# Four subtractions of 128x1024 a pair on GpSimd instead of eight of 128x512, and route steps in halves

## The chip, the cores and the metric

One core of a Trainium2 chip runs the whole kernel. The time is device microseconds of one execution, from its start to its end; a profile of one execution lists every instruction of five engines: TensorE (PE, its weight loads as PEld), VectorE (DVE), ScalarE (ACT), GpSimd (POOL) and SyncE (SP), which only issues DMAs.

## What is computed

The reference takes `x` of 8 x 512 x 128 and computes two blocks, each with a layernorm before it and a residual after it. The first is attention with 16 heads of 64 (here with a second norm inside), the second a mixture of 64 experts, of which each token takes 8, and a shared one:

```python
x = x + attn(layernorm(x))          # scores = q.k / 8 ; attn = softmax(scores) ; ctx = attn.v ; post-norm
x = x + ffn(layernorm(x))           # route: sigmoid scores, top 4 of 8 groups, top 8 experts, weights
                                    # h = silu(x Wg) * (x Wu) * coef ; sum over experts of h Wd, plus shared
```

Products are made of 16-bit parts: a value is kept as a high part and a low part (the rest), and one product is three matmuls, high by high, high by low and low by high.

## The kernel before

The attention goes by **pairs**: 8 batches of 512 tokens by 8 pairs of heads, 64 pairs in all, numbered 0 to 63. Each engine has its own program, written out by hand; an iteration `p` of it has four slots `s` = 0 to 3, and semaphores join the engines. Pairs 0 to 11 and 28 to 63 are written out, pairs 12 to 27 are a loop (on PE and SP all are written out).

What happens to the numerators of the softmax, around which the change lies:

- PE makes the scores of pair `p` in eight pieces of 128x512 (`scores(j)`, j = 2 x key tile + head), ACT takes the exponential of each from the bank into `num` (`exponential(j)`, L723) and counts `exp_done`.
- GpSimd's `lo(s)` (L570) subtracts from `num` its upper 16 bits (`num_hi`, the same words read as bf16 with a stride of two) and writes the rest as f16 into `num_lo`. One `lo(s)` is the key tile `s`, two heads; with its second half it counts `lo_pool`.
- PE's `context(0)` of the **next** iteration multiplies by `v`; before key tile `k` it waits for `lo_pool` of that tile (`pe.wait_ge(lo_pool, 4 * (p - 1) + k + 1)`). What stands ahead of it in PE's order since the last scores of pair `p`: the product with Wo, maxima, one score piece and one projection.
- `num` and `num_lo` are rings of two pairs.

GpSimd's other work in a pair is `split_weights` after `lo(3)` (L583 or L587, by turns), and in some pairs a step of the route of block 0.

DVE makes in each pair four row maxima (L1046), the low parts of q and k (L1055), the low part of a context (L1100, 128x512, both inputs in SBUF; it belongs to pair `p - 2`), two normalisations (L1069, L1071), the low part of v (L1106) and one sum (L1085). L1100 stands behind the second row maximum of slot 2.

The **route of block 0** (layernorms, router, top 8) is spread over pairs 36 to 63 by tables: `DVE_0 = {(pair, slot): ((step, part), ...)}`, and likewise `POOL_0`, `ACT_0` and `PE_0`. `EARLY` is a place in slot 0 of DVE ahead of `low(0)`. Part `None` is a whole step, 0 and 1 are its halves (step 16: eight parts). Step 15 adds one and takes the reciprocal (128x256), step 14 on GpSimd waits for it.

The experts follow, 33 tiles for each of 8 blocks of tokens. While block `n` runs, the route of block `n + 1` is done, at the tile numbers of the tables `DVE_1`, `POOL_1`, `ACT_1`, `PE_1` (block 0) and `DVE_N`, ... (the others).

Of the kernel before, what the change touches and what calls it, by code (L numbers as in the profile page):

```python
# [18 lines left out]
P = 128  # L19
# [3 lines left out]
ALU = mybir.AluOpType  # L23
# [7 lines left out]
QT = S // P  # L31
TOK = B * S
NT = TOK // P
E, G, TOPG, TOPK = 64, 8, 4, 8
EG = E // G
# [14 lines left out]
EARLY = 4  # L50
# [1 line left out]

DVE_0 = {(36, EARLY): ((1, 0),), (36, 1): ((1, 1),), (37, 1): ((2, 0),), (38, EARLY): ((2, 1),), (38, 1): ((3, None),),
         (44, EARLY): ((7, 0),), (44, 1): ((7, 1),), (45, EARLY): ((8, None),), (48, 1): ((12, 0), (12, 1)),
         (50, EARLY): ((15, 0),), (50, 1): ((15, 1),), (52, EARLY): ((16, 0),), (52, 1): ((16, 1),), (53, EARLY): ((16, 2),),
         (53, 1): ((16, 3),), (54, EARLY): ((16, 4),), (54, 1): ((16, 5),), (55, EARLY): ((16, 6),), (55, 1): ((16, 7),),
         (56, EARLY): ((19, None),), (56, 1): ((20, 0), (20, 1)), (57, EARLY): ((21, 0),), (57, 1): ((21, 1),), (58, 1): ((23, None),),
         (59, EARLY): ((24, 0),), (59, 1): ((24, 1),), (60, EARLY): ((25, 0),), (60, 1): ((25, 1),), (61, EARLY): ((26, 0),),
         (61, 1): ((26, 1),), (62, EARLY): ((27, 0),), (62, 1): ((27, 1), (28, None))}
POOL_0 = {(37, 1): (2,), (39, 1): (3,), (42, 1): (5,), (43, 1): (6,), (45, 1): (8,), (51, 1): (14,)}  # L60
ACT_0 = {(40, 3): (4,), (41, 3): (5,), (46, 3): (9,), (47, 3): (10,), (48, 0): (11,), (49, 0): (14,), (63, 0): (30,)}
PE_0 = {(48, 0): (8,), (49, 0): (11,), (63, 0): (27,)}
# [6 lines left out]
PE_N = {8: (8,), 10: (11,), 25: (27,)}  # L69


DVE_1 = {2: (1,), 3: (2,), 4: (3,), 9: (7,), 10: (8,), 14: (12,), 18: (16,), 19: (17,), 20: (18,), 21: (19, 20), 22: (21,),
         23: (23,), 24: (24,), 25: (25,), 26: (26,), 27: (27,), 28: (28,)}
POOL_1 = {4: (3, 2), 6: (5,), 7: (6,), 10: (8,), 16: (14,)}
ACT_1 = {5: (4,), 6: (5,), 11: (9, 10), 14: (11,), 16: (14,), 31: (30,)}
PE_1 = {10: (8,), 12: (11,), 26: (27,)}


PE_TAIL_UP = {2: ((64, 0), (64, 1)), 3: ((64, 2), (64, 3))}
# [5 lines left out]
def layer(nc, x, Wq, bq, Wk, bk, Wv, bv, Wo, bo, gamma, beta, router_w, e_bias,  # L85
          Wg, Wu, Wd, SWg, SWu, SWd, out):
    with ExitStack() as ctx:  # L87
        def sem(name):
            return ctx.enter_context(nc.semaphore(name))
# [6 lines left out]
        def take(words, at=None):  # L96

            if at is None:
                at = top[0]
                top[0] += words  # L100
                assert top[0] <= ARENA, top[0]
            return arena[:, at:at + words]

        def f16(ap):
            return ap.bitcast(F16)
# [27 lines left out]
        num = num_flat.rearrange("p (r t h q) -> p r t h q", r=2, t=QT, h=2)  # L133
        num_hi = num_flat.bitcast(BF16).rearrange("p (r t h q w) -> p r t h q w", r=2, t=QT, h=2, w=2)
        numlo_at = top[0]
        num_lo = f16(take(2 * QT * 2 * S // 2)).rearrange("p (r t h q) -> p r t h q", r=2, t=QT, h=2)
# [27 lines left out]
        def tiles4(ap):  # L164
            return ap.rearrange("p (t d) -> p t d", t=QT)
# [78 lines left out]
        exp_done = sem("exp_done")  # L244
        lo_pool = sem("lo_pool")
        ctx_ps = sem("ctx_ps")
# [22 lines left out]
        sigm = sem("sigm")  # L269
# [25 lines left out]
        def halves(ap):  # L295
            rows = ap.rearrange("p t d -> p (t d)")
            return [rows[:, i * QT * E:(i + 1) * QT * E] for i in range(2)]
# [12 lines left out]
        def scores(m):  # L310
            return tiles4(halves(xin[0])[0] if m == 0 else scores_n)
# [20 lines left out]
        def wait(eng, s, value):  # L332

            if isinstance(value, int) and value <= 0:
                return
            eng.wait_ge(s, value)  # L336
# [4 lines left out]
        def valid(pair, off=0):  # L341

            return not isinstance(pair, int) or 0 <= pair + off < PAIRS
# [11 lines left out]
        def batch_of(u, batch, off):  # L355

            return (u + off) % HP, batch + (u + off) // HP
# [143 lines left out]
        def _(pool):  # L501
# [24 lines left out]
            def constants():  # L526

                pool.memset(post_eps, POST_EPS).then_inc(pool_const, 1)
                pool.memset(ln_eps, LN_EPS).then_inc(pool_const, 1)
                pool.memset(minus_one, -1.0).then_inc(pool_const, 1)  # L530
                pool.wait_ge(pool_const, 9)
# [31 lines left out]
            def run(p, u, batch):  # L563
                def lo(s):

                    for h in range(2):
                        pool.wait_ge(exp_done, 8 * p + 2 * s + h + 1)
                        if s == 0 and h == 0:
                            wait(pool, ctx_ps, 2 * (p - 2) + 2)
                        last = pool.tensor_tensor(num_lo[:, u % 2, s, h, :], num[:, u % 2, s, h, :],  # L570
                                                  num_hi[:, u % 2, s, h, :, 1], ALU.subtract)
                    last.then_inc(lo_pool, 1)

                def split_weights():

                    v, vb = batch_of(u - u % 2, batch, 2)
                    tile, half = vb * (HP // 2) + v // 2, vb * (HP // 4) + v // 4
                    dst = slice(tile, tile + 1) if isinstance(tile, int) else bass.ds(tile, 1)
                    raw = w_raw[:, v // 2 % 2:v // 2 % 2 + 1, :, :]
                    if u % 2 == 0:  # L580
                        pool.wait_ge(w_in[v // 2 % 2], (half + 1) * 48)
                        pool.wait_ge(pool_const, 6)
                        pool.tensor_copy(w_hi[:, dst, :, :], raw).then_inc(w_hi_done, 1)  # L583
                    else:
                        pool.wait_ge(w_hi_done, tile + 1)
                        pool.wait_ge(pool_const, 6)
                        pool.tensor_tensor(w_lo[:, dst, :, :], raw, w_hi[:, dst, :, :],  # L587
                                           ALU.subtract).then_inc(w_split, 1)

                for s in range(4):  # L590
                    if valid(p) and not (isinstance(p, int) and p == PAIRS - 1):
                        lo(s)
                    if isinstance(p, int) and (p, s) == (ROUTE_0, 1):
                        constants()
                    for k in block_0_at(POOL_0, p, s):
                        route(0, 0, k)
                if not isinstance(p, int) or -2 <= p - u % 2 < PAIRS:
                    split_weights()
# [12 lines left out]
            def run_block(n, r, last):  # L611
                for k in range(1, TILES if last else TILES + 1):
                    if not last:
                        for part in (POOL_N if n else POOL_1).get(k, ()):
                            route(n + 1, 1 - r, part)
# [7 lines left out]
        def _(act):  # L623
# [167 lines left out]
            def run_block(n, r, last):  # L791
                for k in range(1, TILES if last else TILES + 1):
# [6 lines left out]
                    if not last:  # L799
                        for part in (ACT_N if n else ACT_1).get(k, ()):  # L800
                            route(n + 1, 1 - r, part)
# [10 lines left out]
        def _(dve):  # L812
# [97 lines left out]
            def route(m, r, k, part=None):  # L910

                def own(ins):

                    ins.then_inc(route_step, 1)
                    n_route[0] += 1
# [8 lines left out]
                first_half, second_half = part != 1, part != 0  # L924
                some = range(QT if first_half and second_half else QT // 2) if first_half else range(QT // 2, QT)
# [25 lines left out]
                if k == 12:  # L951
                    dve.wait_ge(tr_c_hi, m + 1)
                    at = slice(some[0] * P, (some[-1] + 1) * P)
                    last = nc.vector.tensor_tensor(fT_lo[r][:, at], bank_c(m)[:, at], fT_hi[r][:, at], ALU.subtract)
# [2 lines left out]

                work1, work2, work3, work4 = work(m)
                if k == 15:
                    if first_half:  # L960
                        dve.wait_ge(logit_exp, 1)
                        nc.vector.tensor_scalar(scores(m), scores(m), 1.0, None, ALU.add).then_inc(logit_sum, 1)
                    if second_half:
                        dve.wait_ge(logit_sum, 1)
                        nc.vector.reciprocal(scores(m), scores(m)).then_inc(sigm, 1)

                g8 = sfc(m).rearrange("p t (g e) -> p (t g) e", g=G)
                n4, n2, n1 = QT * G * 4, QT * G * 2, QT * G
# [2 lines left out]
                hi1, mid1, lo1, sec1, gsum, rank = (work1[:, i * n1:(i + 1) * n1] for i in range(6))  # L971
# [36 lines left out]
                        settled()  # L1008
                        own(nc.vector.tensor_scalar(rank, rank, -2.0e38, None, ALU.is_lt))
                if k == 23:  # L1010
                    own(nc.vector.tensor_tensor(work4.rearrange("p (n e) -> p n e", e=EG), g8,
                                                rank.unsqueeze(2).broadcast_to([P, QT * G, EG]), ALU.mult))
                if k == 24:
                    for t in some:
                        own(nc.vector.max(best[:, t, :], masked[:, t, :]))
# [132 lines left out]
            def run_block(n, r, last):  # L1148
                if n == 0:
                    tail(run, DVE_TAIL[0])  # L1150
                if not last:
                    for part in (DVE_N if n else DVE_1).get(0, ()):
                        route(n + 1, 1 - r, part)
                for k in range(1, TILES if last else TILES + 1):
# [7 lines left out]
                    if not last:  # L1162
                        for part in (DVE_N if n else DVE_1).get(k, ()):
                            route(n + 1, 1 - r, part)
# [8 lines left out]
        def _(pe):  # L1173
# [262 lines left out]
            def run_block(n, r, last):  # L1436
                for k in range(1, TILES if last else TILES + 1):
# [5 lines left out]
                    if not last:  # L1443
                        for part in (PE_N if n else PE_1).get(k, ()):
                            route(n + 1, 1 - r, part)
# [53 lines left out]
```

## Time and profile before

| | |
|---|---|
| median of 3 runs | 1255.48 us (1254.57 to 1255.91) |
| the profiled execution | 1255.55 us, its span 1253.8 us |
| PE busy | 1220.3 us of the span |
| GpSimd busy | 991.7 us, of which L570 538.0 us in 504 instructions |
| DVE, ACT busy | 1066.4 us, 885.6 us |
| granted clock of TensorE | 0.989 on average; 1.00 from 50 us on |

The attention takes the span from 36 us to about 707 us, the experts the rest. A timeline row gives start, duration, engine, line, operation, target and source, and in brackets the idle time of the engine before it with what ended it. Rows of GpSimd that follow each other closely overlap a little: the next starts 0.04 us before the end of the last.

### The profile page before, as it was taken

Reading aid. Unit: us, or ns where it says so; the run is one execution under the profiler, and the core shown is the slowest. Engines: PE = TensorE matmul, PEld = TensorE weight load, DVE = VectorE, ACT = ScalarE, POOL = GpSimd, SP = SyncE. Lnnn points to the kernel's source line nnn. Section 1 sums busy time; section 2 is a strip of 40 time slices with the busy share of each in tenths; the row PEclk is TensorE's granted clock in tenths of the full one; section 3 lists DMA queues with packets and bytes.
Section 4 is the critical chain, followed back from the end, with each engine's and each line's share of the span. In section 5 each row is a group of like instructions: output and inputs, shape, how many; then the busy total and the mean of one; then the engine's idle time right before and its main releaser. Section 6 shows DMA issues by size and latency. Waiting matters only on the chain. (4 is left out here: it accounts for less than half of the span.)

```text
span 1253.8 us, 33479 instructions
## 1 busy us (share of the span) xinstructions
PE 1220.3 (97%) x12473; PEld 684.3 (55%) x12473; DVE 1066.4 (85%) x1965; ACT 885.6 (71%) x1586; POOL 991.7 (79%) x1218
## 2 busy tenths in 40 slices
PE   3999999999999999999999999999999999999998
PEld 0466666666666666666666644444444444444443
DVE  6788988888888998989999888787888878787875
ACT  4788877777777778787777666666667676667554
POOL 2788888888888999988888576868786877777665
PEclk7899999999999999999999999999999999999999
DMA  7455564665554655654565354444444444444442
GB/s 185 103 105 113 96 119 107 111 109 113 106 115 107 120 108 116 109 115 109 109 115 110 69 141 130 142 139 142 138 145 134 141 138 142 136 129 138 139 143 85
DMA packets 186862, 152.60 MB, mean 122 GB/s; under 512 B 104720, under 2 KB 143952, under 8 KB 186704
## 3 DMA queue, kind: packets, MB, share of 16 engines
q1 hardware_dynamic: 186704, 150.50, 51.1%
q8 instruction: 99, 1.62, 0.5%
q14 instruction: 59, 0.48, 0.1%
HBM read 80.16 MB, written 3.15 MB: 66 GB/s over the span
## 5 line engine op out<-in xcount | busy, mean ns | idle before, releaser
L1175 PE MATMUL bank<-arena 128*128 128x65 f16 (+2 forms) x12344 | 1209.9, 263 | 20.5 <-DVE arena L1055 7.1
L1175 PEld LDWEIGHTS bank<-arena 128*128 128x128 f16 (+1 forms) x12344 | 669.5, 98 | 548.5 <-issue 85.6
L570 POOL TENSOR_TENSOR arena<-arena 128x512 f16<-128x512 f32 x504 | 538.0, 1093 | 82.1 <-ACT arena L723 81.7
L608 POOL TENSOR_TENSOR arena<-arena 128x256 f16<-128x256 f32 x528 | 342.4, 675 | 132.3 <-ACT arena L784 125.7
L723 ACT ACTIVATE arena<-bank 128x512 f32<-128x512 f32 x512 | 291.8, 595 | 120.9 <-PE bank L1175 104.1
L1046 DVE TENSOR_REDUCE arena<-bank 128x2 f32<-128x1024 f32 x256 | 311.8, 1219 | 43.1 <-PE bank L1175 43.0
L1140 DVE TENSOR_TENSOR arena<-arena,bank 128x512 f32<-128x512 f32 x264 | 181.9, 689 | 61.9 <-ACT bank L779 38.9
L784 ACT ACTIVATE arena<-arena 128x512 f16<-128x512 f32 x264 | 164.7, 624 | 95.9 <-DVE arena L1140 94.0
L1132 DVE TENSOR_TENSOR arena<-arena,bank 128x512 f32<-128x512 f32 x256 | 173.9, 679 | 24.2 <-PE bank L1175 23.2
L779 ACT ACTIVATE bank<-bank 128x512 f32<-128x512 f32 x264 | 153.3, 581 | 55.3 <-PE bank L1175 55.1
L1055 DVE SCALAR_TENSOR_TENSOR arena<-bank,arena 128x512 f16<-128x512 f32 x128 | 95.5, 746 | 19.4 <-ACT arena L713 19.3
L713 ACT ACTIVATE arena<-bank,arena 128x512 f16<-128x512 f32 x128 | 87.9, 687 | 20.7 <-PE bank L1175 16.3
L748 ACT ACTIVATE arena<-bank 2x1024 f16<-2x1024 f32 x64 | 65.0, 1015 | 11.0 <-PE bank L1175 10.8
L1100 DVE TENSOR_TENSOR arena<-arena 128x512 f16<-128x512 f32 x64 | 63.6, 994 | 2.6 <-ACT arena L756 2.6
L1071 DVE TENSOR_TENSOR arena<-bank,arena 128x256 f32<-128x256 f32 x128 | 54.3, 425 | 4.4
L1106 DVE TENSOR_TENSOR arena<-bank,arena 128x512 f16<-128x512 f32 x64 | 43.6, 681 | 0.5 <-ACT arena L764 0.5
L1085 DVE TENSOR_TENSOR arena<-bank,arena 128x512 f32<-128x512 f32 (+1 forms) x64 | 43.6, 681 | 0.0
L756 ACT ACTIVATE arena<-arena 128x512 f16<-128x512 f32 x64 | 39.8, 622 | 3.5 <-DMA arena<-arena 3.5
L764 ACT ACTIVATE arena<-bank 128x512 f16<-128x512 f32 x64 | 39.1, 611 | 0.0
L587 POOL TENSOR_TENSOR arena<-arena 128x384 f16<-128x384 f32 (+1 forms) x33 | 30.2, 915 | 0.2
L740 ACT ACTIVATE arena<-arena 128x8 f16<-128x8 f32 x64 | 13.5, 210 | 23.8 <-DVE arena L1046 23.7
L1069 DVE RECIPROCAL arena<-bank 128x4 f32<-128x4 f32 x128 | 22.8, 178 | 4.1 <-PE bank L1175 2.8
(106 smaller groups left out, 368.0 us busy)
## 6 DMA issues: line engine op xcount, KB each, us to landing
arena<-coef_rows SPq DMA_DIRECT2D x512, 128.0 KB, 2.9
arena<-arena SPq DMA_DIRECT2D x256, 128.0 KB, 2.5
arena<-arena SPq DMA_DIRECT2D x64, 256.0 KB, 3.1
arena<-in_L_attn_x SPq DMA_DIRECT2D x9, 256.0 KB, 3.5
arena<-in_L_ffn_Wg SPq DMA_DIRECT2D x32, 64.0 KB, 2.4
arena<-in_L_ffn_Wu SPq DMA_DIRECT2D x32, 64.0 KB, 2.2
arena<-in_L_ffn_Wd SPq DMA_DIRECT2D x32, 64.0 KB, 2.2
arena<-arena SPq DMA_TRANSPOSE x128, 3.4
```

Of the source, the lines that this page charges most:

```text
L570: last = pool.tensor_tensor(num_lo[:, u % 2, s, h, :], num[:, u % 2, s, h, :], num_hi[:, u % 2, s, h, :, 1], ALU.subtract)
L608: last = pool.tensor_tensor(hid_lo[:, r, at], hid[:, r, at], hid_hi[:, r, at], ALU.subtract)
L713: nc.scalar.activation(flat[:, (u + 3) % 2, (ZQH, ZKH)[which], :], proj_bank(t, which), ACT.Identity, bias=bias[:, n:n + 1]).then_inc(qk_h ...
L723: nc.scalar.activation(num[:, u % 2, j // 2, j % 2, :], ps_st[ST_BANK[j]], ACT.Exp).then_inc(exp_done, 1)
L748: nc.scalar.activation(stack[K:K + 2, (u + 1) % 4, :, Q2, :], ps_turn[K:K + 2, :].unsqueeze(1).broadcast_to([2, 2, S]), ACT.Copy).then_inc ...
L779: nc.scalar.activation(ps_gate[r % 3], ps_gate[r % 3], ACT.Silu).then_inc(silu_done, 1)
L784: nc.scalar.activation(hid_hi[:, r, :], hid[:, r, :], ACT.Copy).then_inc(hid_hi_done, 1)
L1046: nc.vector.tensor_reduce(rmax[:, up % 2, q, :], max_bank(pair, q).rearrange("p (h k) -> p h k", h=2), AX.X, ALU.max).then_inc(max_done, 1)
L1055: nc.vector.scalar_tensor_tensor(out=flat[:, (u + 3) % 2, (ZQL, ZKL)[which], :], in0=proj_bank(t, which), scalar=(bq8, bk_c)[which][:, n:n ...
L1132: nc.vector.tensor_tensor(prod[:, i % 2, :], coef_b[:, j % 4, :], ps_up[i % 3], ALU.mult).then_inc(prod_done, 1)
L1140: nc.vector.tensor_tensor(hid[:, i % 6, :], prod[:, i % 2, :], ps_gate[i % 3], ALU.mult).then_inc(hid_done, 1)
L1175: return nc.tensor.matmul(out_, lhsT, rhs, start=start, stop=stop, skip_group_check=True)
```

## The change

`lo(s)` becomes one instruction over both heads, 128x1024, which waits for the exponential of the second head; before, each head had an instruction and a wait of its own. Step 15 of block 0 gets three parts, the reciprocal in two halves of 128x128, in pairs 50 and 51. Step 23 of block 0 is halved, step 28 moves by a slot. In `DVE_1`, `POOL_1`, `ACT_1` and `PE_1` steps 4 to 14 move by one tile (step 4 from tile 5 to 6, and so on).

```diff
-         (50, EARLY): ((15, 0),), (50, 1): ((15, 1),), (52, EARLY): ((16, 0),), ...
+         (50, EARLY): ((15, 0),), (50, 1): ((15, 1),), (51, EARLY): ((15, 2),), (52, EARLY): ((16, 0),), ...
...
-POOL_1 = {4: (3, 2), 6: (5,), 7: (6,), 10: (8,), 16: (14,)}
+POOL_1 = {4: (3, 2), 7: (5,), 8: (6,), 11: (8,), 17: (14,)}
...
-                    for h in range(2):
-                        pool.wait_ge(exp_done, 8 * p + 2 * s + h + 1)
-                        if s == 0 and h == 0:
-                            wait(pool, ctx_ps, 2 * (p - 2) + 2)
-                        last = pool.tensor_tensor(num_lo[:, u % 2, s, h, :], num[:, u % 2, s, h, :],
-                                                  num_hi[:, u % 2, s, h, :, 1], ALU.subtract)
-                    last.then_inc(lo_pool, 1)
+                    pool.wait_ge(exp_done, 8 * p + 2 * s + 2)
+                    if s == 0:
+                        wait(pool, ctx_ps, 2 * (p - 2) + 2)
+                    pool.tensor_tensor(num_lo[:, u % 2, s, :, :], num[:, u % 2, s, :, :],
+                                       num_hi[:, u % 2, s, :, :, 1], ALU.subtract).then_inc(lo_pool, 1)
...
                 if k == 15:
-                    if first_half:
+                    if part == 0:
                         dve.wait_ge(logit_exp, 1)
                         nc.vector.tensor_scalar(scores(m), scores(m), 1.0, None, ALU.add).then_inc(logit_sum, 1)
-                    if second_half:
+                    else:
+                        half = scores(m)[:, (part - 1) * QT // 2:part * QT // 2, :]
                         dve.wait_ge(logit_sum, 1)
-                        nc.vector.reciprocal(scores(m), scores(m)).then_inc(sigm, 1)
+                        last = nc.vector.reciprocal(half, half)
+                        if part == 2:
+                            last.then_inc(sigm, 1)
```

GpSimd's order in two of the written-out pairs before, with the semaphores each waits for (L583 and L587 are `split_weights`, L570 is `lo`):

```order
L583 CAST arena<-arena 128x384 [waits pool_const,w_in0]
L570 TENSOR_TENSOR arena<-arena 128x512 [waits ctx_ps,exp_done]
L570 TENSOR_TENSOR arena<-arena 128x512 [waits exp_done] x7
L587 TENSOR_TENSOR arena<-arena 128x384 [waits pool_const,w_hi_done]
L570 TENSOR_TENSOR arena<-arena 128x512 [waits ctx_ps,exp_done]
```

The same place now (L581 and L585 are `split_weights`, L569 is `lo`):

```order
L581 CAST arena<-arena 128x384 [waits pool_const,w_in1]
L569 TENSOR_TENSOR arena<-arena 128x1024 [waits ctx_ps,exp_done]
L569 TENSOR_TENSOR arena<-arena 128x1024 [waits exp_done] x3
L585 TENSOR_TENSOR arena<-arena 128x384 [waits pool_const,w_hi_done]
L569 TENSOR_TENSOR arena<-arena 128x1024 [waits ctx_ps,exp_done]
```

Nothing else moves on GpSimd in the attention: four instructions with four waits stand where eight with eight stood.

DVE's order from slot 1 of pair 50 on, before (L965 is the reciprocal of step 15, L1046 a row maximum, L1055 `low`, L1085 the sum):

```order
L965 RECIPROCAL arena<-arena 128x256
L1046 TENSOR_REDUCE arena<-bank 128x2
L1055 SCALAR_TENSOR_TENSOR arena<-bank,arena 128x512
L1046 TENSOR_REDUCE arena<-bank 128x2
L1100 TENSOR_TENSOR arena<-arena 128x512
L1069 RECIPROCAL arena<-bank 128x4
L1071 TENSOR_TENSOR arena<-bank,arena 128x4x64
L1106 TENSOR_TENSOR arena<-bank,arena 128x512
L1046 TENSOR_REDUCE arena<-bank 128x2
L1085 TENSOR_TENSOR arena<-bank,arena 128x512
L1055 SCALAR_TENSOR_TENSOR arena<-bank,arena 128x512
```

And now (L964 is the reciprocal; the other lines stand two further down in the file than before):

```order
L964 RECIPROCAL arena<-arena 128x128
L1048 TENSOR_REDUCE arena<-bank 128x2
L1057 SCALAR_TENSOR_TENSOR arena<-bank,arena 128x512
L1048 TENSOR_REDUCE arena<-bank 128x2
L1102 TENSOR_TENSOR arena<-arena 128x512
L1071 RECIPROCAL arena<-bank 128x4
L1073 TENSOR_TENSOR arena<-bank,arena 128x4x64
L1108 TENSOR_TENSOR arena<-bank,arena 128x512
L1048 TENSOR_REDUCE arena<-bank 128x2
L1087 TENSOR_TENSOR arena<-bank,arena 128x512
L964 RECIPROCAL arena<-arena 128x128
L1057 SCALAR_TENSOR_TENSOR arena<-bank,arena 128x512
```

Half of the reciprocal has moved ten instructions on, into slot 0 of pair 51.

## Rows read from the trace of the kernel before

**Rows 1.** The page, part 1: busy time of each engine.

```profile
PE 1220.3 (97%) x12473; PEld 684.3 (55%) x12473; DVE 1066.4 (85%) x1965; ACT 885.6 (71%) x1586; POOL 991.7 (79%) x1218
```

**Rows 2.** Windows: length, then busy PE, PEld, DVE, ACT, POOL; clock, DMA share, GB/s.

```profile
40.00:705.00 665.00, 661.94 (x9605) 424.49 (x9603) 596.69 (x901) 512.83 (x919) 582.62 (x580) 1.00 0.56 108
720.00:1170.00 450.00, 447.69 (x2247) 209.49 (x2246) 373.96 (x891) 299.76 (x544) 340.75 (x531) 1.00 0.46 138
```

**Rows 3.** Timeline, ACT: the first exponential of pairs 38 to 41.

```profile
441.65 0.60 ACT L723 ACTIVATE arena<-bank 128x512 f32<-128x512 f32 x1 [1.21 <-PE bank L1175]
...
452.19 0.60 ACT L723 ACTIVATE arena<-bank 128x512 f32<-128x512 f32 x1 [1.21 <-PE bank L1175]
...
462.73 0.60 ACT L723 ACTIVATE arena<-bank 128x512 f32<-128x512 f32 x1 [1.21 <-PE bank L1175]
...
473.44 0.60 ACT L723 ACTIVATE arena<-bank 128x512 f32<-128x512 f32 x1 [0.45 <-PE bank L1175]
```

**Rows 4.** Timeline, GpSimd: last four subtractions of pair 38, then of pair 39.

```profile
448.34 4.49 POOL L570 TENSOR_TENSOR arena<-arena 128x512 f16<-128x512 f32 x4 [1.18 <-ACT arena L723]
...
458.03 1.02 POOL L541 TENSOR_TENSOR arena<-arena 128x4 f32<-128x4 f32 x1
...
459.28 4.48 POOL L570 TENSOR_TENSOR arena<-arena 128x512 f16<-128x512 f32 x4
```

**Rows 5.** Groups of GpSimd by form: count, busy us, mean ns, idle before.

```profile
L570 POOL TENSOR_TENSOR arena<-arena 128x512 f16<-128x512 f32 x504 | 538.0, 1093 | 82.1 <-ACT arena L723 81.7
...
L547 POOL TENSOR_TENSOR arena<-arena 128x512 f32<-128x512 f32 x8 | 10.2, 1280 | 0.0
...
L556 POOL TENSOR_TENSOR arena<-arena 128x256 f32<-128x256 f32 x8 | 5.8, 724 | 2.8 <-PE bank L1175 1.6 <-ACT arena L696 1.2
...
L543 POOL TENSOR_TENSOR arena<-arena 128x4 f32<-128x4 f32 x16 | 3.2, 201 | 1.3
```

**Rows 6.** Timeline, GpSimd: pieces 4, 5 and 7 of pair 30.

```profile
363.69 1.04 POOL L570 TENSOR_TENSOR arena<-arena 128x512 f16<-128x512 f32 x1 [1.18 <-ACT arena L723]
...
364.70 1.48 POOL L570 TENSOR_TENSOR arena<-arena 128x512 f16<-128x512 f32 x1
...
367.14 1.04 POOL L570 TENSOR_TENSOR arena<-arena 128x512 f16<-128x512 f32 x1
```

**Rows 7.** Timeline, ACT: exponentials 5 and 7 of pair 30.

```profile
364.03 0.59 ACT L723 ACTIVATE arena<-bank 128x512 f32<-128x512 f32 x1
...
365.73 0.60 ACT L723 ACTIVATE arena<-bank 128x512 f32<-128x512 f32 x1
```

**Rows 8.** Timeline, DVE: L1100 in pair 30 and in pair 58.

```profile
364.31 0.97 DVE L1100 TENSOR_TENSOR arena<-arena 128x512 f16<-128x512 f32 x1
...
662.26 0.68 DVE L1100 TENSOR_TENSOR arena<-arena 128x512 f16<-128x512 f32 x1
```

**Rows 9.** Timeline of ACT, DVE and GpSimd in pair 24, inside the loop.

```profile
300.81 0.59 ACT L723 ACTIVATE arena<-bank 128x512 f32<-128x512 f32 x1
...
301.02 1.03 DVE L1100 TENSOR_TENSOR arena<-arena 128x512 f16<-128x512 f32 x1
...
300.47 4.49 POOL L570 TENSOR_TENSOR arena<-arena 128x512 f16<-128x512 f32 x4 [1.18 <-ACT arena L723]
```

**Rows 10.** Timeline: first exponentials of pairs 50 and 51, the reciprocal, PE's wait.

```profile
569.24 0.60 ACT L723 ACTIVATE arena<-bank 128x512 f32<-128x512 f32 x1 [1.21 <-PE bank L1175]
...
573.16 1.74 DVE L965 RECIPROCAL arena<-arena 128x256 f32<-128x256 f32 x1
...
576.04 0.39 PE L1175 MATMUL bank<-arena 128*128 128x512 f16 x1 [0.82 <-DVE arena L1046]
...
580.76 0.60 ACT L723 ACTIVATE arena<-bank 128x512 f32<-128x512 f32 x1 [1.21 <-PE bank L1175]
```

**Rows 11.** Waits: PE for L570 (us in total, times, longest).

```profile
PE bank L1175 <- POOL arena L570: 0.9, 2, 0.6
```

**Rows 12.** The page, part 5: DVE's row maxima.

```profile
L1046 DVE TENSOR_REDUCE arena<-bank 128x2 f32<-128x1024 f32 x256 | 311.8, 1219 | 43.1 <-PE bank L1175 43.0
```

More of the change, by code:

```diff
@@ L54 @@
          (44, EARLY): ((7, 0),), (44, 1): ((7, 1),), (45, EARLY): ((8, None),), (48, 1): ((12, 0), (12, 1)),
-         (50, EARLY): ((15, 0),), (50, 1): ((15, 1),), (52, EARLY): ((16, 0),), (52, 1): ((16, 1),), (53, EARLY): ((16, 2),),
+         (50, EARLY): ((15, 0),), (50, 1): ((15, 1),), (51, EARLY): ((15, 2),), (52, EARLY): ((16, 0),), (52, 1): ((16, 1),), (53, EARLY): ((16, 2),),
          (53, 1): ((16, 3),), (54, EARLY): ((16, 4),), (54, 1): ((16, 5),), (55, EARLY): ((16, 6),), (55, 1): ((16, 7),),
-         (56, EARLY): ((19, None),), (56, 1): ((20, 0), (20, 1)), (57, EARLY): ((21, 0),), (57, 1): ((21, 1),), (58, 1): ((23, None),),
+         (56, EARLY): ((19, None),), (56, 1): ((20, 0), (20, 1)), (57, EARLY): ((21, 0),), (57, 1): ((21, 1),), (58, EARLY): ((23, 0),), (58, 1): ((23, 1),),
          (59, EARLY): ((24, 0),), (59, 1): ((24, 1),), (60, EARLY): ((25, 0),), (60, 1): ((25, 1),), (61, EARLY): ((26, 0),),
-         (61, 1): ((26, 1),), (62, EARLY): ((27, 0),), (62, 1): ((27, 1), (28, None))}
+         (61, 1): ((26, 1),), (62, EARLY): ((27, 0),), (62, 1): ((27, 1),), (62, 2): ((28, None),)}
 POOL_0 = {(37, 1): (2,), (39, 1): (3,), (42, 1): (5,), (43, 1): (6,), (45, 1): (8,), (51, 1): (14,)}
@@ L69 @@
 PE_N = {8: (8,), 10: (11,), 25: (27,)}
-DVE_1 = {2: (1,), 3: (2,), 4: (3,), 9: (7,), 10: (8,), 14: (12,), 18: (16,), 19: (17,), 20: (18,), 21: (19, 20), 22: (21,),
+DVE_1 = {2: (1,), 3: (2,), 4: (3,), 10: (7,), 11: (8,), 15: (12,), 18: (16,), 19: (17,), 20: (18,), 21: (19, 20), 22: (21,),
          23: (23,), 24: (24,), 25: (25,), 26: (26,), 27: (27,), 28: (28,)}
-POOL_1 = {4: (3, 2), 6: (5,), 7: (6,), 10: (8,), 16: (14,)}
-ACT_1 = {5: (4,), 6: (5,), 11: (9, 10), 14: (11,), 16: (14,), 31: (30,)}
-PE_1 = {10: (8,), 12: (11,), 26: (27,)}
+POOL_1 = {4: (3, 2), 7: (5,), 8: (6,), 11: (8,), 17: (14,)}
+ACT_1 = {6: (4,), 7: (5,), 12: (9, 10), 15: (11,), 17: (14,), 31: (30,)}
+PE_1 = {11: (8,), 13: (11,), 26: (27,)}
 PE_TAIL_UP = {2: ((64, 0), (64, 1)), 3: ((64, 2), (64, 3))}
@@ L1010, in route @@
                 if k == 23:
-                    own(nc.vector.tensor_tensor(work4.rearrange("p (n e) -> p n e", e=EG), g8,
-                                                rank.unsqueeze(2).broadcast_to([P, QT * G, EG]), ALU.mult))
+                    at = slice(some[0] * G, (some[-1] + 1) * G)
+                    own(nc.vector.tensor_tensor(work4.rearrange("p (n e) -> p n e", e=EG)[:, at, :], g8[:, at, :],
+                                                rank[:, at].unsqueeze(2).broadcast_to([P, len(some) * G, EG]), ALU.mult))
                 if k == 24:
```

## The prediction

> **What bounds the kernel now.** I read the busy times first, then stretches of the span, then single pairs. PE is busy 1220.3 of 1253.8 us [rows 1]; in the attention 661.94 of 665.00 us, in the experts 447.69 of 450.00 us, at a granted clock of 1.00 [rows 2]. GpSimd is the next busiest there only after DVE, with 582.62 us of 665.00. So PE sets the pace, and a pair costs what PE's own instructions cost: its first exponential starts 10.54 us after that of the pair before (441.65 to 452.19 to 462.73 [rows 3]). Less work on GpSimd gives PE nothing back, since in the whole run PE stands visibly still for L570 twice, 0.9 us together [rows 11]. What can matter is when the last subtraction of a pair ends, because PE needs it in the next iteration.
>
> How much later may it end? The trace has a trial of it. In pair 38 the last piece ends at 448.34 + 4.49 = 452.83, which is 11.18 us after that pair's first exponential. In pair 39 a route step on GpSimd (L541, 1.02 us) stands ahead, and the last piece ends at 459.28 + 4.48 = 463.76, 11.57 us after 452.19 [rows 3, 4]: 0.39 us later. The next distance of first exponentials is 473.44 - 462.73 = 10.71 instead of 10.54, so PE lost 0.17 us. About 0.22 us of delay is free, the rest is paid one to one. And it is paid in every pair in which it happens: what GpSimd waits for comes from PE, so a late subtraction delays PE, which delays the next exponentials by the same.
>
> **The change part by part.**
>
> *The length of a piece.* No row shows 128x1024. A piece of 512 alone takes 1.04 us [rows 6]. An instruction of 4 elements takes 0.20 us; of the f32 forms, 512 and 256 elements take 1.28 and 0.72 us, which puts 0.17 us outside the elements [rows 5]. So 0.17 to 0.20 of the 1.04 us is there once per instruction, and a merged piece saves that: 2 x 1.04 - 0.19 = 1.89 us. The bounds are 1.88 (all of the 0.20 saved) and 2.04 (nothing saved; two pieces back to back, which overlap by 0.04). I take 1.89, which both neighbours give. GpSimd's busy time falls by about 252 x 0.15 = 38 us, all of it time in which PE didn't wait.
>
> *When the last piece ends, written-out pairs.* Pair 30 as it is: exponential 5 ends at 364.03 + 0.59 = 364.62, piece 4 (started 363.69, after exponential 4) ends at 364.73, piece 5 ends at 366.18, piece 7 at 368.18 [rows 6, 7]. Piece 5 takes 1.48 us instead of 1.04, and that is L1100: DVE starts it at 364.31 while piece 4 runs, and it ends at 365.28, 0.55 us after piece 4; piece 5 ends 0.90 us after L1100 [rows 6, 8]. The two don't overlap: DVE stood until piece 4 was done, then piece 5 until L1100 was done, with 0.14 us of its 1.04 already behind it. The Trainium skill has a rule on these two ("SBUF — State Buffer", section "SBUF: two separate sides"): GpSimd and a VectorE instruction with two SBUF inputs share a port pair, whichever starts first holds it for the whole instruction. The trace agrees, with the 0.97 us of L1100 and the 1.48 us beside it. The rule speaks against the change, since one hold by GpSimd grows from 1.04 to 1.89 us; a sum by that is a rival below.
>
> Now the new order. Pieces 2 and 3 used to end at 363.69 - 1.18 = 362.51. The first two merged pieces start where piece 1 did, with the second head's exponential, and take 3.74 instead of 3.04 us: they end near 363.2. The third must wait for exponential 5, so GpSimd is idle when L1100 comes at 364.31. L1100 runs at once, 0.68 us as in pair 58 where it hardly waited [rows 8], to 364.99. The third piece, released at 364.70, is held until then and ends at 364.99 + 1.89 - 0.14 = 366.74. The fourth starts 0.04 us earlier, at 366.70 (exponential 7 ended at 366.33 [rows 7], so it isn't what holds it), and ends at 368.59. That is 0.41 us later than 368.18; 0.22 are free, so PE loses 0.19 us a pair.
>
> The reason in a word: half of the old work of key tile 2 was done before exponential 5 was there. Now none of it can be, and the saved 0.19 us a piece doesn't make up for it.
>
> *In the loop.* Pair 24: exponential 5 ends at 301.40, L1100 starts at 301.02, the last piece ends at 300.47 + 4.49 = 304.96 [rows 9]. New: L1100 to 301.70, third piece to 303.45, fourth to 305.30, 0.34 us later; PE loses 0.12 us.
>
> *Behind the later piece* on GpSimd stand `split_weights` and the first piece of the next pair. The next first piece waits for its own exponentials, over a microsecond later, and the weights are needed by the experts alone, so nothing else is late. The waits for the second head in the first two pieces cost nothing: PE takes tiles 0 and 1 a whole iteration later.
>
> *Reciprocal.* In pair 50 it holds DVE for 1.74 us, PE stands 0.82 us for the row maximum behind it, and the pair takes 580.76 - 569.24 = 11.52 us [rows 10]. In halves DVE is late by some 0.9 us less at that place, which is the whole wait. Pair 50 becomes a pair like the others: 10.54 + 0.19 - 11.52 = -0.79 us. The second half, in slot 0 of pair 51, stands ahead of a `low` and a row maximum; DVE has idle time there in the mean (43.1 us over 64 pairs, 0.67 a pair [rows 12]), and a rest of 0.2 us disappears in PE's new wait.
>
> *Other steps of the route.* Step 23 in halves and step 28 a slot later: the same DVE work. The steps of block 1, one tile later: PE's whole idle time from 720 to 1170 us is 2.3 us [rows 2], so not more than that can be gained; a GpSimd step of 1.28 us [rows 5] put ahead of an awaited tile would cost at most about that. I take 0.
>
> *Sum.* Written-out pairs 3 to 11 and 28 to 59 without pair 50: 40 x 0.19 = 7.6. Loop, pairs 12 to 27: 16 x 0.12 = 1.9. Pairs 1, 2 and 60 to 62: the last three have no projection ahead of the context, so no slack, and pay up to 0.41 each; five pairs at 0.3 make 1.5. Pair 50: -0.8. Together +10.2 us on the profiled execution's 1255.55 (span 1253.8 and 1.75 around it), which is 0.07 from the median of the runs: 1265.7 us, 0.8% slower.
>
> **The rivals.**
>
> *The hold by L1100 costs nothing* (GpSimd gets the port at once or L1100 shifts away). Then the third piece ends at 364.70 + 1.89 = 366.59, the fourth at 368.44, 0.26 us late, 0.04 paid: 56 x 0.04 + 5 x 0.2 - 0.95 = +2.3, so 1257.9 us. For it: DVE will have a little more idle time. Against it: 0.44 us of hold in piece 5 in pair after pair, and L1100's start is bound to PE like everything else.
>
> *It is faster or nothing changes*: the slack is larger than 0.22 us or the merged piece shorter than 1.78 us. Then the pairs stay at 10.54 us, PE's own work, and only pair 50 gains: 1255.55 - 0.98 = 1254.6 us. A gain of more than 2.5 us would need other waits to vanish with it, which only the experts' 2.3 us could supply. Against it: 0.20 us is all that an instruction can save.
>
> *Merged pieces save nothing*, 2.04 us each. The last piece is another 0.30 us later: 40 x 0.49 + 16 x 0.42 + 5 x 0.6 - 0.5 = +28.8, so 1284 us. The Trainium skill ("GPSIMD Engine Reference", section "Elementwise — side-by-side cycle accounting") gives 4497 ns for a two-input add over 2048 f32 and about 2.5 cycles an element as a floor; an estimate from it is 2.25 us a piece, and about 1310 us. The trace differs for this form: 1.04 us for 512 elements is below that floor, so the row decides.
>
> *DVE is shut out by a long piece.* If L1100 came after the third piece's start, 0.39 us later than now (364.31 against 364.70), it would wait to 366.59 and end at 367.14 instead of 365.28. DVE would be 1.86 us late a pair against 0.67 idle [rows 12], 1.2 us a pair over 60 pairs: about 1327 us. The port rule named above speaks for this one: a lock held for 1.89 us is worse to meet than one of 1.04. Against it: both starts hang on the same PE work, so the 0.39 us should stay. In pairs 36 to 62 single route steps on DVE may meet a long piece; that is inside my range.
>
> **How the numbers follow.** Forecast 0.60; no hold 0.18; nothing or faster 0.10; nothing saved 0.07; DVE shut out 0.05. A measurement of this kernel tells about 0.2%, 2.5 us, from no change. Slower: the forecast, the two slow rivals and 0.08 of the second case, whose 1257.9 lies on the border: 0.80. The same: 0.10 of it and half of the third: 0.15. Faster: 0.05. The likeliest case's own range is 1261 to 1271 (0.03 us more or less a piece moves a pair by 0.06, the sum by 4). The range for all, 1257 to 1277, takes in the second case and half of the way to pieces that save nothing.
>
> **What would show it.** GpSimd's group of 252 instructions of 128x1024 at about 1.9 us, held ones a little longer; L1100 near 0.68 us instead of 0.97; first exponentials 10.73 us apart in the written-out pairs and 10.66 in the loop; pair 50 no longer at 11.52. PE's new waits are so short that few will be listed as idle time. It would be wrong if the pairs stayed at 10.54, or if the third piece ran 1.9 us from its release with L1100 at 0.97 or more.

## The result, and the profile after

The changed kernel takes 1265.93 us (median of 4 runs, 1265.41 to 1266.27) against 1255.70 of the kernel before: a ratio of 1.0083, 95% interval 1.0071 to 1.0096. The forecast was 1265.7. The profiled execution took 1266.27 us, its span 1264.5, which is 10.7 us more than before.

The page's busy times, to set beside [rows 1]:

```profile
PE 1229.1 (97%) x12473; PEld 687.7 (54%) x12473; DVE 1049.1 (83%) x1967; ACT 889.3 (70%) x1586; POOL 938.1 (74%) x966
```

GpSimd is busy 54 us less, DVE 17 us less, and the kernel is slower. Neither engine's busy time was what the time hung on. The attention's stretch (columns as in [rows 2]) hardly shows it either: PE is idle for 675.00 - 670.16 = 4.84 us of it, against 3.06 us before.

```profile
40.00:715.00 675.00, 670.16 (x9602) 427.80 (x9600) 577.63 (x898) 515.96 (x919) 527.77 (x328) 1.00 0.54 106
```

The loss shows in the distance of pairs. First exponentials of pairs 30 and 31 (written out), 24 and 25 (loop), 50 and 51, from the timeline of ACT:

```profile
361.63 0.60 ACT L721 ACTIVATE arena<-bank 128x512 f32<-128x512 f32 x1 [1.21 <-PE bank L1177]
...
372.36 0.60 ACT L721 ACTIVATE arena<-bank 128x512 f32<-128x512 f32 x1 [1.21 <-PE bank L1177]
...
297.50 0.60 ACT L721 ACTIVATE arena<-bank 128x512 f32<-128x512 f32 x1 [1.15 <-PE bank L1177]
...
308.17 0.60 ACT L721 ACTIVATE arena<-bank 128x512 f32<-128x512 f32 x1 [1.15 <-PE bank L1177]
...
577.76 0.60 ACT L721 ACTIVATE arena<-bank 128x512 f32<-128x512 f32 x1 [1.21 <-PE bank L1177]
...
588.49 0.60 ACT L721 ACTIVATE arena<-bank 128x512 f32<-128x512 f32 x1 [1.21 <-PE bank L1177]
```

10.73 us written out, 10.67 in the loop, 10.73 for pair 50; before it was 10.54, 10.54 and 11.52 [rows 3, 10]. Inside pair 30, the third and fourth merged piece, DVE's L1102 (L1100 before) and exponential 5:

```profile
369.52 2.05 POOL L569 TENSOR_TENSOR arena<-arena 128x1024 f16<-128x1024 f32 x1 [1.53 <-ACT arena L721]
...
371.53 1.89 POOL L569 TENSOR_TENSOR arena<-arena 128x1024 f16<-128x1024 f32 x1
...
369.13 0.68 DVE L1102 TENSOR_TENSOR arena<-arena 128x512 f16<-128x512 f32 x1
...
368.85 0.59 ACT L721 ACTIVATE arena<-bank 128x512 f32<-128x512 f32 x1
```

A piece alone takes 1.89 us, as forecast; the third is held to 2.05 by L1102, which comes first and takes 0.68 instead of 0.97 us [rows 8]. The last piece ends at 373.42, 3.98 us after exponential 5 (369.44). Before it was 368.18 - 364.62 = 3.56 [rows 6, 7]: 0.42 us later, of which 0.19 shows in the distance of pairs. (From the pair's first exponential, at 361.63, the last piece is 0.61 us later than before. The other 0.19 is the stop of the pair before: it lies ahead of exponential 5 and isn't lateness of GpSimd.) GpSimd now waits 1.53 us for exponential 5, in front of the chain that matters.

The list of waits hides nearly all of it. PE for L569 (us in total, times, longest), to set beside [rows 11]:

```profile
PE bank L1177 <- POOL arena L569: 1.9, 6, 0.7
```

Six waits of 1.9 us are listed, while some sixty pairs each lost 0.13 to 0.19 us. The ends of matmuls are modelled, and the small ones of `context` overlap in the listing, so most of a short stop is hidden. The matmul that needs pair 30's last piece starts 0.06 us after the piece's end (373.42), and the row ahead of it ends at 372.53 + 0.92 = 373.45:

```profile
372.53 0.92 PE L1177 MATMUL bank<-arena 128*128 128x512 f16 x19
...
373.48 0.29 PE L1177 MATMUL bank<-arena 128*128 128x65 f16 x4
```

A stop of 0.19 us shows as a gap of 0.03 us, too short for the list. The distance of a repeating event is the view that shows such a loss.

Where the 10.7 us are, by the distances of first exponentials in the two timelines:

| stretch | longer by, us | the forecast's term |
|---|---|---|
| pairs 3 to 11 | 2.0 | 9 x 0.19 = 1.7 |
| pairs 12 to 27 (loop) | 2.2 | 16 x 0.12 = 1.9 |
| pairs 28 to 59 without 50 | 5.7 | 31 x 0.19 = 5.9 |
| pair 50 | -0.8 | -0.8 |
| pairs 1, 2 and 60 to 62 | 1.7 | 1.5 |
| start, pair 63, experts | -0.1 | 0 |

### The profile page after: what moved, and what is told of

It is laid out like the page before. It is cut to its first block and busy times, and to the rows that moved or that the text cites. A ratio compares the mean times of both kernels' runs of the same rounds, so it can differ in the third digit from the quotient of the medians.

```text
span 1264.5 us, 33165 instructions
## 1 busy us (share of the span) xinstructions
PE 1229.1 (97%) x12473; PEld 687.7 (54%) x12473; DVE 1049.1 (83%) x1967; ACT 889.3 (70%) x1586; POOL 938.1 (74%) x966
## 5 line engine op out<-in xcount | busy, mean ns | idle before, releaser
L569 POOL TENSOR_TENSOR arena<-arena 128x1024 f16<-128x1024 f32 x252 | 481.4, 1929 | 146.9 <-ACT arena L721 145.8
L1048 DVE TENSOR_REDUCE arena<-bank 128x2 f32<-128x1024 f32 x256 | 311.7, 1218 | 51.1 <-PE bank L1177 50.7
L1102 DVE TENSOR_TENSOR arena<-arena 128x512 f16<-128x512 f32 x64 | 44.1, 688 | 4.1 <-ACT arena L754 4.1
L585 POOL TENSOR_TENSOR arena<-arena 128x384 f16<-128x384 f32 (+1 forms) x33 | 30.3, 920 | 0.2
L681 ACT ACTIVATE arena<-arena 128x128 f32<-128x128 f32 x32 | 13.3, 482 | 17.1 <-POOL arena L543 17.1
```

Of the source, the lines that this page charges most:

```text
L569: pool.tensor_tensor(num_lo[:, u % 2, s, :, :], num[:, u % 2, s, :, :], num_hi[:, u % 2, s, :, :, 1], ALU.subtract).then_inc(lo_pool, 1)
L1048: nc.vector.tensor_reduce(rmax[:, up % 2, q, :], max_bank(pair, q).rearrange("p (h k) -> p h k", h=2), AX.X, ALU.max).then_inc(max_done, 1)
```

## The experiments

### Each half of the change alone

The first is the kernel before with the merged `lo` and nothing else of the change:

```diff
-                    for h in range(2):
-                        pool.wait_ge(exp_done, 8 * p + 2 * s + h + 1)
...
+                    pool.wait_ge(exp_done, 8 * p + 2 * s + 2)
...
```

The second is the changed kernel with the old `lo`:

```diff
-                    pool.wait_ge(exp_done, 8 * p + 2 * s + 2)
...
+                    for h in range(2):
+                        pool.wait_ge(exp_done, 8 * p + 2 * s + h + 1)
...
```

> The kernel before with the merged subtractions alone; tables and reciprocal as before. Theory (the late last piece is the whole loss, the route tables bring only pair 50's 0.8 to 1.0 us): 1266.6 us, pairs 10.73 us apart (loop 10.66), pair 50 still the longest at 11.3 to 11.7. Rival (the moved route steps cost part of the 10 us): clearly under 1265, the pairs between 10.54 and 10.73.

> The change without the merging: eight subtractions of 128x512 a pair, but the new tables, the reciprocal in halves and step 23 in halves. Theory: pairs 10.54 us apart as before, pair 50 too, so 1255.55 - 0.98 = 1254.6 us. Rival (the moved steps cost something themselves): 1257 us or more, with new waits of PE between pair 36 and the first 20 tiles of experts.

The merging alone took 1267.25 us, 1.0101 of before (1.0084 to 1.0117); the tables alone 1254.69 us, 0.9998 (0.9989 to 1.0008). So all of the loss comes with the merging, and what the tables bring is under what whole runs can tell. In the traces the pairs of the first stand 10.73 us apart (10.67 in the loop), those of the second 10.54. Pair 50 takes 11.33 us in the first and 578.70 - 567.98 = 10.72 us in the second:

```profile
567.98 0.60 ACT L723 ACTIVATE arena<-bank 128x512 f32<-128x512 f32 x1 [1.22 <-PE bank L1179]
...
578.70 0.60 ACT L723 ACTIVATE arena<-bank 128x512 f32<-128x512 f32 x1 [1.22 <-PE bank L1179]
```

That is 0.18 us over the 10.54 that was expected of it. In the whole change pair 50 takes 10.73, like its neighbours: there this rest of the reciprocal's cost and the 0.19 us of the late piece don't add up. The tables also cost something that was expected to be free: pair 62 takes 8.92 us with them alone and 8.59 before.

With the merging alone, pair 50 shows something the forecast had only as a rival. DVE is late there from the long reciprocal, and L1098 (its L1100) comes after the third piece has started:

```profile
585.77 1.90 POOL L569 TENSOR_TENSOR arena<-arena 128x1024 f16<-128x1024 f32 x1 [1.56 <-ACT arena L721]
...
586.09 2.12 DVE L1098 TENSOR_TENSOR arena<-arena 128x512 f16<-128x512 f32 x1
```

It stands until the piece ends at 587.67 and finishes 0.54 us later: 2.12 us instead of 0.68. This is DVE shut out by a long piece, in one pair of this kernel. In the whole change the halved reciprocal keeps DVE from being so late, and it doesn't occur in pair 50.

### Which merged piece costs

Both are the changed kernel with a `lo(s)` that does some tiles in one subtraction and the others in two. The first merges tiles 0, 1 and 3, the second tile 2 alone (there the condition is `s in (2,)`):

```diff
+                    if s in (0, 1, 3):
+                        pool.wait_ge(exp_done, 8 * p + 2 * s + 2)
...
+                    else:
+                        for h in range(2):
+                            pool.wait_ge(exp_done, 8 * p + 2 * s + h + 1)
...
```

> The change, but key tile 2 again in two subtractions of 128x512; tiles 0, 1 and 3 stay merged. Theory (the loss is the head start lost on tile 2 before exponential 5): piece 4 starts with exponential 4 again, tile 2 is done 366.18 - 357.00 = 9.18 us after the pair's first exponential as before, the merged tile 3 is released by exponential 7 (9.33 + 0.08) and ends at 11.30, 0.12 later than before and inside the 0.22 of slack: pairs 10.54 us apart, about 1255.0 us. Rival (every merged piece costs by its own length or its late release): three quarters of the loss, about 1263 us, pairs at 10.68.

> The change, but only key tile 2 merged; tiles 0, 1 and 3 in two subtractions each. Theory: tile 2 ends 9.74 us after the pair's first exponential, the two halves of tile 3 follow back to back and take 2.00 instead of 1.85: the last ends 0.56 us later than before in the written-out pairs and 0.49 in the loop, of which 0.34 and 0.27 are paid. Slower than the whole change: pairs about 10.88 us apart (loop 10.81), 40 x 0.34 + 16 x 0.27 + some 2 - 0.6 = +19, about 1275 us. Rival (cost by merged piece): a quarter of the loss, about 1257 us.

Tile 2 merged alone: 1274.41 us, 1.0158 (1.0141 to 1.0175), and slower than all four merged. Three merged but not tile 2: 1257.09 us, 1.0017 (1.0008 to 1.0027). A cost by the number of merged pieces would have had them the other way round. GpSimd and first exponentials of pairs 30 and 31 with tile 2 merged alone:

```profile
365.40 0.60 ACT L730 ACTIVATE arena<-bank 128x512 f32<-128x512 f32 x1 [1.21 <-PE bank L1186]
...
376.27 0.60 ACT L730 ACTIVATE arena<-bank 128x512 f32<-128x512 f32 x1 [1.21 <-PE bank L1186]
...
373.43 2.05 POOL L570 TENSOR_TENSOR arena<-arena 128x1024 f16<-128x1024 f32 x1 [1.97 <-ACT arena L730]
...
375.44 2.03 POOL L577 TENSOR_TENSOR arena<-arena 128x512 f16<-128x512 f32 x2
```

and the same with tile 2 in two pieces:

```profile
358.26 0.60 ACT L730 ACTIVATE arena<-bank 128x512 f32<-128x512 f32 x1 [1.21 <-PE bank L1186]
...
368.80 0.60 ACT L730 ACTIVATE arena<-bank 128x512 f32<-128x512 f32 x1 [1.21 <-PE bank L1186]
...
364.95 1.04 POOL L577 TENSOR_TENSOR arena<-arena 128x512 f16<-128x512 f32 x1 [0.53 <-ACT arena L730]
...
365.95 1.48 POOL L577 TENSOR_TENSOR arena<-arena 128x512 f16<-128x512 f32 x1
...
367.66 1.89 POOL L570 TENSOR_TENSOR arena<-arena 128x1024 f16<-128x1024 f32 x1 [0.22 <-ACT arena L730]
```

Merged, tile 2 starts 373.43 - 365.40 = 8.03 us after the first exponential and the pair takes 10.87 us. In two, it starts at 6.69 as before and the pair takes 10.54, although the last piece, merged, ends 0.12 us later than before: that is inside the slack. The head start of one piece before exponential 5 is what the change gave away.

The kernel with tile 2 in two pieces was expected at 1255.0 and is about 2 us over it. Its ordinary pairs lose nothing; by the distances of first exponentials 1.5 us come in pairs 36 to 49, 0.8 in pairs 60 to 62 (0.3 of them with the tables alone) and 0.6 in pairs 1 to 3. Pair 39 shows how: its merged first tiles end later, a route step (L541) comes after them, and the last piece runs from 463.66 to 465.55, 11.89 us after the pair's first exponential at 453.66.

```profile
453.66 0.60 ACT L730 ACTIVATE arena<-bank 128x512 f32<-128x512 f32 x1 [1.21 <-PE bank L1186]
...
460.21 1.02 POOL L541 TENSOR_TENSOR arena<-arena 128x4 f32<-128x4 f32 x1
...
463.66 1.89 POOL L570 TENSOR_TENSOR arena<-arena 128x1024 f16<-128x1024 f32 x1
...
464.20 0.60 ACT L730 ACTIVATE arena<-bank 128x512 f32<-128x512 f32 x1 [1.22 <-PE bank L1186]
...
475.22 0.60 ACT L730 ACTIVATE arena<-bank 128x512 f32<-128x512 f32 x1 [0.45 <-PE bank L1186]
```

That is 0.71 us later than the 11.18 of an ordinary pair, and the next distance is 475.22 - 464.20 = 11.02, 0.48 over 10.54. My expectation had overlooked the route's pairs.

### The hold by L1102

In the first, L1102 becomes a memset; in the second it is moved to slot 3, behind the low part of v.

```diff
-                            nc.vector.tensor_tensor(ctx_l, ctxn[:, u % 2, :, :].rearrange("p t c -> p (t c)"),
-                                                    ctx_h, ALU.subtract).then_inc(ctx_lo, 1)
+                            nc.vector.memset(ctx_l, 0.0).then_inc(ctx_lo, 1)
```

```diff
                                                     v_hi[:, u % 2, :, :, 0:K], ALU.subtract).then_inc(v_lo_done, 1)
+                        if valid(p, -2) and not (isinstance(p, int) and p >= PAIRS):
+                            dve.wait_ge(ctx_hi, p - 2 + 1)
+                            nc.vector.tensor_tensor(ctx_l, ctxn[:, u % 2, :, :].rearrange("p t c -> p (t c)"),
+                                                    ctx_h, ALU.subtract).then_inc(ctx_lo, 1)
```

> The change, but DVE's L1102 (two SBUF inputs) replaced by a memset of its target at the same place: the low part of the contexts is left out, as zeros. Theory (0.15 of the 0.41 us by which the last piece is late is the hold by L1102): the third merged piece runs 1.89 us instead of 2.05 (1.98 in the loop), the last piece ends 0.26 us later than before the change instead of 0.41 (loop 0.34), 0.04 is paid: pairs 10.58 us apart in loop and written-out pairs, 40 x 0.15 + 16 x 0.08 + about 0.5 = 7.8 us less than the change: 1258 us. Rival (the piece is longer for a reason of its own, the port is not shared): third piece stays at 2.05, about 1266 us.

> The change, but L1102 moved on DVE from the end of slot 2 to the end of slot 3, behind L1108, so that it comes while the third merged piece runs. Theory (whichever comes first keeps the port for its whole instruction; a form of the rival in which DVE is shut out): the third piece runs 1.89 us without hold, L1102 stands until its end and takes about 1.1 us instead of 0.68, the fourth piece is then held by L1102 and takes about 2.3 us; the last piece ends 0.7 us later than before the change, 0.49 is paid: pairs 11.0 us apart, 1282 to 1288 us. Rival (a hold costs the same wherever it falls): 1266 us.

Without it: 1257.6 us, 1.0019 (1.0009 to 1.0028). GpSimd and ACT in pair 30:

```profile
366.56 1.90 POOL L569 TENSOR_TENSOR arena<-arena 128x1024 f16<-128x1024 f32 x1 [1.53 <-ACT arena L721]
...
368.41 1.90 POOL L569 TENSOR_TENSOR arena<-arena 128x1024 f16<-128x1024 f32 x1
...
358.82 0.60 ACT L721 ACTIVATE arena<-bank 128x512 f32<-128x512 f32 x1 [1.21 <-PE bank L1176]
...
369.40 0.60 ACT L721 ACTIVATE arena<-bank 128x512 f32<-128x512 f32 x1 [1.21 <-PE bank L1176]
```

Both pieces run 1.90 us and the pair takes 10.58, the expected number. Of the loss of 0.19 us a pair, 0.15 is the hold.

Moved behind the low part of v: 1289.4 us, 1.027 (1.0252 to 1.0287), with pairs 381.82 - 370.80 = 11.02 us apart. GpSimd and DVE in pair 30, then ACT:

```profile
378.98 1.89 POOL L569 TENSOR_TENSOR arena<-arena 128x1024 f16<-128x1024 f32 x1 [1.53 <-ACT arena L721]
...
380.83 2.34 POOL L569 TENSOR_TENSOR arena<-arena 128x1024 f16<-128x1024 f32 x1
...
380.73 0.69 DVE L1113 TENSOR_TENSOR arena<-arena 128x512 f16<-128x512 f32 x1
...
370.80 0.60 ACT L721 ACTIVATE arena<-bank 128x512 f32<-128x512 f32 x1 [1.22 <-PE bank L1181]
...
381.82 0.60 ACT L721 ACTIVATE arena<-bank 128x512 f32<-128x512 f32 x1 [1.21 <-PE bank L1181]
```

The hold has moved from the third piece to the fourth and is larger, 2.34 us, as expected: a hold between the two last pieces costs its full 0.45 us. The wait of 1.1 us expected of DVE was wrong for the ordinary pairs: the instruction arrives only 0.14 us before the third piece ends, and takes 0.69. The stops of PE are long enough here to be listed (60 waits for L569), but 0.17 us of each stays hidden: pairs that lost 0.49 us list 0.32.

```profile
PE bank L1181 <- POOL arena L569: 21.2, 60, 1.3
```

The total is just above the 1282 to 1288 expected. Two pairs in which DVE is late lie behind that, and the first shows what a long shut-out costs. In pair 36 L1113 comes just after the fourth piece has started and stands until that piece ends at 448.97:

```profile
445.21 3.76 POOL L569 TENSOR_TENSOR arena<-arena 128x1024 f16<-128x1024 f32 x2 [1.31 <-ACT arena L721]
...
447.12 2.39 DVE L1113 TENSOR_TENSOR arena<-arena 128x512 f16<-128x512 f32 x1
...
450.70 10.53 PE L1181 MATMUL bank<-arena 128*128 128x512 f16 x148 [1.22 <-DVE arena L1048]
...
448.21 0.60 ACT L721 ACTIVATE arena<-bank 128x512 f32<-128x512 f32 x1 [1.21 <-PE bank L1181]
...
460.14 0.60 ACT L721 ACTIVATE arena<-bank 128x512 f32<-128x512 f32 x1 [1.22 <-PE bank L1181]
```

It takes 2.39 us instead of 0.69. The row maximum behind it (L1048) is late, PE stands for that, and the distance is 460.14 - 448.21 = 11.93 us: 1.39 over the 10.54 of before, where its neighbours lose 0.48. In pair 61 L1113 again takes 2.39 us, and pair 62 is 3.8 us longer than before; how much of that the shut-out makes wasn't taken apart.

### A step moved out of the way

The new tables with `lo` in eight pieces, as in the second kernel, and:

```diff
-POOL_0 = {(37, 1): (2,), (39, 1): (3,), (42, 1): (5,), (43, 1): (6,), (45, 1): (8,), (51, 1): (14,)}
+POOL_0 = {(37, 1): (2,), (39, 3): (3,), (42, 1): (5,), (43, 1): (6,), (45, 3): (8,), (51, 1): (14,)}
```

> The new tables with eight subtractions of 128x512 a pair, and the two route steps of four small GpSimd instructions (steps 3 and 8) moved from slot 1 to slot 3 of pairs 39 and 45, behind the last subtraction. Theory (the last subtraction late by more than 0.22 us is what costs): the pairs after 39 and 45 lose their extra 0.17 us each, 0.35 us in all, about 1254.3 us; too little for the clock of whole runs, but the distances of first exponentials go from 10.71 to 10.54 us. Rival (the split of weights and the next pair's first pieces, which these steps then delay, are late instead): pairs 40 and 46 at 10.6 us or more.

1254.65 us, 0.9995 of before (0.9986 to 1.0005), no gain over the tables alone. Pairs 40 and 46 do go from 10.71 to 10.53 us, but the pairs after them take 10.76. Here the rival was right, one pair further on. GpSimd in pair 40, and the first exponentials of pairs 40 to 42:

```profile
463.64 1.02 POOL L541 TENSOR_TENSOR arena<-arena 128x4 f32<-128x4 f32 x1
...
465.76 8.47 POOL L570 TENSOR_TENSOR arena<-arena 128x512 f16<-128x512 f32 x8
...
462.62 0.60 ACT L723 ACTIVATE arena<-bank 128x512 f32<-128x512 f32 x1 [1.22 <-PE bank L1179]
...
473.15 0.60 ACT L723 ACTIVATE arena<-bank 128x512 f32<-128x512 f32 x1 [0.45 <-PE bank L1179]
...
483.91 0.60 ACT L723 ACTIVATE arena<-bank 128x512 f32<-128x512 f32 x1 [0.45 <-PE bank L1179]
```

The eight pieces of pair 40 run without a break and end at 474.23, 11.61 us after 462.62 and 0.43 later than usual, so the distance after it is 10.76. GpSimd's idle 1.18 us before piece 4 was too little for a step of 1.6 us. No kernel here beats the one before by more than runs can tell.

## Why the prediction was right

The steps held one by one. The merged piece was put at 1.89 us and measured 1.89. L1102 was to run at once in 0.68 us and hold the third piece; it did, 2.05 us against the 2.04 that the forecast's times give (366.74 - 364.70). The last piece was to end 0.41 us later, and ended 0.42 later; the pair was to grow by 0.19 us and grew by 0.19. In the loop 0.12 was forecast and 0.13 came. Pair 50 gave back 0.79 as summed, though partly by luck: the prediction took the whole wait for the long reciprocal as gone, while the tables alone leave 0.18 us of it, and only together with the 0.19 of the late piece does this rest cost nothing more.

The term on which all rests, 0.22 us of slack and one to one beyond it, was read from a single disturbed pair, and the runs confirm it at six more lengths: a last piece later by 0.12 costs nothing (tile 2 split), 0.27 costs 0.04 (no hold), 0.42 costs 0.19 (the change), 0.56 costs 0.34 (tile 2 merged alone), 0.71 costs 0.48 (L1102 moved), and in pair 39 of the kernel with tile 2 split 0.71 costs 0.48 too.

Of the rivals, "the hold costs nothing" was forecast at 1257.9 us, and the kernel without the hold took 1257.6. "Merged pieces save nothing" fell with the 1.89 us. So did the estimate of 2.25 us a piece, which the prediction works out from the Trainium skill ("GPSIMD Engine Reference", section "Elementwise — side-by-side cycle accounting"); the floor of about 2.5 cycles an element stands in the section "Instruction dispatch" of the same reference in the Trainium skill, and the section named here gives about 2.6. "DVE is shut out" happens where DVE is late enough: in pair 50 of the merging alone and in pairs 36 and 61 with L1102 moved, but not in the attention pairs of the change. Its price of 1.2 us a pair was of the right size: pair 36 led to 1.39.

Three sizes were off without moving the total much. Pairs 3 to 27 came to 4.2 instead of 3.6 us: the loop lost 0.13 a pair, its first pair 0.19, as a late piece shows one distance later, and pair 3 alone 0.42. Nothing in the forecast foresaw pair 3. The runs show that it has no slack, since it loses the whole lateness in every kernel with merged pieces: 0.11, 0.27, 0.42, 0.56 and 0.71 us where the last piece is later by 0.12, 0.27, 0.42, 0.56 and 0.71. What in PE's order takes the slack away there stays open.

Pairs 1, 2 and 60 to 62 came to 1.7 us for a forecast of 1.5, and that they came so close is luck. Of the three that were to have no slack, pair 60 lost 0.19 like any other and pair 62 lost 0.84, of which 0.33 comes with the tables alone, a cost that the prediction put at nothing. And the later release of the merged pieces isn't quite free, as the prediction had it: pairs 1 and 2 lost 0.12 and 0.28 us in the change, but nothing and 0.05 where tile 2 alone is merged.

GpSimd's busy time fell by 54 us and not by 38, because the hold in it shrank as well, from 0.44 us a pair to 0.16 (0.09 in the loop).

## What to carry to other kernels

When one engine sets the pace, find the last instruction of each round on the engines that feed it, and measure how much later it may end; a round that was disturbed by chance is a trial that the trace has already run. Merging instructions saves their fixed part but makes the first half wait for the second half's input: count what was done before the last input came, not the busy time. And judge a periodic loop by the distance of one repeating event, because stops of PE of 0.2 us a round didn't appear in the list of waits.

## What the runs showed of the hardware

A GpSimd subtraction and a 128x512 DVE instruction with two SBUF inputs never did their work at the same time, and their listed times contain the waiting. In all nine traces, 310 such DVE instructions came while a subtraction ran, with between 0.09 and 1.84 us of it left. Each ended 0.54 to 0.59 us after the subtraction, so the same L1100 took 0.97, 1.03 or 2.12 us, and 0.68 where it didn't wait. In the other order the merged piece ended 1.75 us after the DVE instruction (59 times in the change), 0.14 us sooner than its own length of 1.89 would give. A reader who takes the mean duration of either for its cost is misled.

What an instruction does to the other engine depends on which comes first. L1113 took 0.69 us where it came at the end of a piece, and 2.39 us where it came at the start of one. So a change of length on one engine can free the other and still make the kernel slower.
